# Scores one step ahead of the weighing in the router's attention of a graph and expert kernel

## What is computed

```
h = (x_flat @ W_gat).reshape(M, HEADS, NUM_EXPERTS)          # HEADS 4, NUM_EXPERTS 4
a_src, a_dst = (h * att_src).sum(-1), (h * att_dst).sum(-1)
e = leaky_relu(a_src[src] + a_dst[dst], negative_slope=0.2)
ee = exp(e - segment_max(e, dst)[dst])
alpha = ee / (segment_sum(ee, dst)[dst] + 1e-16)
agg = segment_sum(h[src] * alpha[:, :, None], dst) + b_gat
scores = layernorm(agg).mean over heads
w = softmax(top 2 of scores)
out = sum over experts of w * (gelu(x @ W1[ei] + b1[ei]) @ W2[ei] + b2[ei])
```

## Time and profile before

| | |
|---|---|
| median of three runs | 5306.82 us (5290.3 to 5312.11) |
| the profiled execution | 5308.64 us, its span 5307.1 us |
| mean granted clock of PE over the span | 0.876 of full speed |
| PE busy | 3317.8 us (63%) |
| DVE busy | 3019.0 us (57%) |
| POOL busy | 2063.6 us (39%) |
| ACT busy | 1600.5 us (30%) |
| exponentials of the router's attention (L2894) | 65 |
| indirect gathers of its rows (L2831) | 352 in 44 octets |

### The profile page before, as it was taken

How to read it: one execution, slowest core, us unless ns; L and a number is a source line. 1 busy time by engine, 2 the same in 40 slices (tenths; PEclk the granted TensorE clock), 3 DMA queues, 4 the chain that set the end, 5 groups by cost and what they waited for, 6 DMA issues and landing times. The chain is left out here.

```text
span 5307.1 us, 71457 instructions
## 1 busy us (share of the span) xinstructions
PE 3317.8 (63%) x17311; PEld 2482.2 (47%) x17312; DVE 3019.0 (57%) x7503; ACT 1600.5 (30%) x2745; POOL 2063.6 (39%) x1895
## 2 busy tenths in 40 slices
PE   0440036499698695277771699868345567777677
PEld 0430036487586584255550244356234445555455
DVE  8886648588588556133335754442444555565563
ACT  0232024376475121133330454322101222222221
POOL 1136300200200252656551200026377877777662
PEclk9999999899898796588885899979677788898899
DMA  0311125443452322211123554422443333333241
GB/s 31 74 19 44 13 82 232 169 153 104 170 159 85 111 67 91 88 27 33 33 38 108 200 170 158 165 91 67 129 91 86 88 86 83 82 84 84 78 76 28
DMA packets 326382, 501.17 MB, mean 94 GB/s; under 512 B 152614, under 2 KB 241005, under 8 KB 324168
## 3 DMA queue, kind: packets, MB, share of 16 engines
q1 hardware_dynamic: 193750, 259.75, 15.6%
q0 software_dynamic: 83888, 189.73, 13.7%
q10 hardware_dynamic: 48578, 49.98, 2.8%
HBM read 367.16 MB, written 137.35 MB: 95 GB/s over the span
## 5 line engine op out<-in xcount | busy, mean ns | idle before, releaser
L2393 POOL DMA_INDIRECT l3a_got<-rows,l3a_idx x832 | 1003.3, 1206 | 356.1 <-issue 257.5
L2469 PE MATMUL ps<-l3a_v,ident 128*128 x2032 | 592.9, 455 | 476.8 <-DVEq L2596 395.3
L2469 PEld LDWEIGHTS ps<-l3a_v,ident 128*128 128x128 f32 x2032 | 452.5, 228 | 614.5 <-issue 522.0
L1659 PE MATMUL ps<-l0a_all_rows,l0a_w 128*128 128x257 f32 x2500 | 559.5, 384 | 38.1 <-DVE l0a_w L1768 37.8
L1659 PEld LDWEIGHTS ps<-l0a_all_rows,l0a_w 128*128 128x128 f32 x2500 | 473.9, 191 | 124.3 <-issue 54.3
L2831 POOL DMA_INDIRECT l1a_got<-rows,l1a_idx x352 | 351.2, 998 | 248.8 <-DVEq L3033 130.0
L2069 PE MATMUL ps<-l2a_table,l2a_count 128*128 128x512 bf16 x1875 | 409.7, 382 | 38.1 <-ACT l2a_count L1994 38.1
L2419 ACT ACT_TABLE_LOAD x90 | 115.5, 1283 | 750.7 <-issue 459.4
L2854 PE MATMUL ps<-xt,l1w_w 128*128 x640 | 225.8, 506 | 169.3 <-ACT l1a_h L2909 74.2
L2069 PEld LDWEIGHTS ps<-l2a_table,l2a_count 128*128 128x128 bf16 x1875 | 183.9, 98 | 264.0 <-issue 46.6
L2590 DVE TENSOR_TENSOR l3a_v<-l3a_got,l3a_p_kept x127 | 291.6, 2296 | 0.0
(11 more groups left out here) (1019 smaller groups left out, 6446.8 us busy)
## 6 DMA issues: line engine op xcount, KB each, us to landing
l0a_held<-counts SPq DMA_DIRECT2D x130, 640.0 KB
counts<-count_held SPq DMA_DIRECT2D x13, 3200.0 KB
l2a_held<-counts SPq DMA_DIRECT2D x65, 640.0 KB
l3a_got<-rows,l3a_idx POOLq DMA_INDIRECT x832
l_y<-l1a_y_sb ACTq DMA_DIRECT2D x20, 640.0 KB
l2a_table<-rows SPq DMA_DIRECT2D x16, 640.0 KB, 5.1
l2a_state<-l1a_fresh ACTq DMA_DIRECT2D x1, 9984.0 KB
l2a_seen<-l2a_state POOLq DMA_DIRECT2D x12, 768.0 KB, 6.0
```

The source lines that it names most:

```text
L1659: ins = pe.matmul(sums_of(n, k, D + 1), w[:, at, k * P:(k + 1) * P], all_rows[:, at, 1:RW], start=(at == 0), stop=(at == HI - 1))
L2393: pool.indirect_dma_start(out=got[:, at:at + RW], out_offset=None, in_=rows[:, :], in_offset=bass.IndirectOffsetOnAxis(ap=idx[:, a, k:k + ...
L2469: ins = pe.matmul(totals, c.ident[:, :], rows_now[:, k, :, :].rearrange("p h d -> p (h d)"), start=(k == 0), stop=(k == ADDED - 1))
```

## The change

`edges` is cut in two, `scores_of` (L3008 to L3014 before) and `values_of` (L3018 to L3027). The scores of the opening step are followed at once by the emptying of PE's outputs. A loop step makes the scores of octet o and then the values of octet o-1; the values of the last octet follow behind the loop. The exponentials lie in `p_kept`, two tiles by turns, chosen by o % 2 in a register. `weighed` becomes `exped`: from the second step on DVE waits for the exponentials before it writes `d` anew, and once more behind the loop. `freed` is counted up behind the multiplication of an octet instead of at the entry of the next step.

```diff
-        e, d, p = (sb(n, [P, SLOTS + 1, H]) for n in ("e", "d", "p"))
+        e, d = (sb(n, [P, SLOTS + 1, H]) for n in ("e", "d"))
+        p_kept = sb("p_kept", [P, 2, SLOTS + 1, H])
...
+        def weights(o, lo, hi):
+
+            return p_kept[:, bass.ds(o % 2, 1), lo:hi, :].rearrange("p o s h -> p (o s) h")
...
-                    def exponentials():
+                    def exponentials(o):
                         act.wait_ge(shifted, 1)
                         act.sem_clear(shifted)
-                        act.activation(p[:, :, :], d[:, :, :], ACT.Exp).then_inc(weighed, 1)
+                        act.activation(weights(o, 0, SLOTS + 1), d[:, :, :], ACT.Exp).then_inc(exped, 1)
...
-                    def edges(o, row):
-                        ch.restart()
+                    def scores_of(o, row, opening):
...
                         ch(dve.tensor_reduce(top[:, :], e[:, :, :].rearrange("p s h -> p h s"), AX, ALU.max))
+                        if not opening:
+                            dve.wait_ge(exped, 1)
+                            dve.sem_clear(exped)
                         ch(dve.tensor_tensor(d[:, :, :], e[:, :, :], top[:, :].unsqueeze(1).broadcast_to([P, SLOTS + 1, H]), ALU.subtract))
                         dve.sem_inc(shifted, 1)
                         ch(dve.tensor_copy(e[:, SLOTS, :], top[:, :]))
 
-                        dve.wait_ge(weighed, 1)
-                        dve.sem_clear(weighed)
+                    def values_of(o, closing):
+
+                        if closing:
+                            dve.wait_ge(exped, 1)
+                            dve.sem_clear(exped)
+                        mine, older = weights(o, 0, SLOTS), weights(o, SLOTS, SLOTS + 1).rearrange("p s h -> p (s h)")
...
-                        ch.add(dve.tensor_tensor(by_head(acc), by_head(acc), spread(p[:, SLOTS, :]), ALU.mult))
+                        ch.add(dve.tensor_tensor(by_head(acc), by_head(acc), spread(older), ALU.mult))
                         ch.join()
-                        ch.add(dve.tensor_tensor(p[:, SLOTS, :], p[:, SLOTS, :], den, ALU.mult))
+                        if not closing:
+                            dve.sem_inc(freed, 1)
+                        ch.add(dve.tensor_tensor(older, older, den, ALU.mult))
...
-                    edges(begins // SLOTS, begins % SLOTS)
+                    first, last = begins // SLOTS, ends // SLOTS
+                    scores_of(first, begins % SLOTS, True)
                     beside()
-                    with dve.Fori(begins // SLOTS + 1, ends // SLOTS + 1) as o:
-                        dve.sem_inc(freed, 1)
-                        edges(o, closing_row(ends, o))
+                    with dve.Fori(first + 1, last + 1) as o:
+                        ch.restart()
+                        scores_of(o, closing_row(ends, o), False)
+                        values_of(o - 1, False)
+                    ch.restart()
+                    values_of(last, True)
```

More of the change, by code:

```diff
@@ L2780, in attend_beside_experts @@
         warmed, warm = sb("warmed", [P, 1]), sem("warm")
-        shifted, weighed, closed, kept, placed = (sem(n) for n in ("shifted", "weighed", "closed", "kept", "placed"))
+        shifted, exped, closed, kept, placed = (sem(n) for n in ("shifted", "exped", "closed", "kept", "placed"))
         product, hidden, used, emptied, y_out = (sem(n) for n in ("product", "hidden", "used", "emptied", "y_out"))
@@ L2889, in attend_tile @@
                 def attend_tile(t, at):
-                    def exponentials():
+                    def exponentials(o):
                         act.wait_ge(shifted, 1)
                         act.sem_clear(shifted)
-                        act.activation(p[:, :, :], d[:, :, :], ACT.Exp).then_inc(weighed, 1)
+                        act.activation(weights(o, 0, SLOTS + 1), d[:, :, :], ACT.Exp).then_inc(exped, 1)
                     begins, ends = stream.bounds(act, t)
-                    exponentials()
+                    exponentials(begins // SLOTS)
                     at(0)
                     with act.Fori(begins // SLOTS + 1, ends // SLOTS + 1) as o:
-                        exponentials()
+                        exponentials(o)
                     at(1)
@@ L3014, in edges @@
                         ch(dve.tensor_copy(e[:, SLOTS, :], top[:, :]))
-                        dve.wait_ge(weighed, 1)
-                        dve.sem_clear(weighed)
+                    def values_of(o, closing):
[3 more added lines that the diff above has]
+                        mine, older = weights(o, 0, SLOTS), weights(o, SLOTS, SLOTS + 1).rearrange("p s h -> p (s h)")
                         ch.add(dve.tensor_tensor(v[:, :, :].rearrange("p s (h d) -> p s h d", h=H),
                                                  buffer(o, 0, VW).rearrange("p s (h d) -> p s h d", h=H),
-                                                 p[:, 0:SLOTS, :].unsqueeze(3).broadcast_to([P, SLOTS, H, DH]), ALU.mult))
-                        ch.add(dve.tensor_tensor(by_head(acc), by_head(acc), spread(p[:, SLOTS, :]), ALU.mult))
+                                                 mine.unsqueeze(3).broadcast_to([P, SLOTS, H, DH]), ALU.mult))
+                        ch.add(dve.tensor_tensor(by_head(acc), by_head(acc), spread(older), ALU.mult))
                         ch.join()
-                        ch.add(dve.tensor_tensor(p[:, SLOTS, :], p[:, SLOTS, :], den, ALU.mult))
+                        if not closing:
+                            dve.sem_inc(freed, 1)
+                        ch.add(dve.tensor_tensor(older, older, den, ALU.mult))
                         ch.add(dve.tensor_reduce(part[:, :], v[:, :, :].rearrange("p s w -> p w s"), AX, ALU.add))
                         ch.join()
-                        ch.add(dve.tensor_reduce(den, p[:, :, :].rearrange("p s h -> p h s"), AX, ALU.add))
+                        ch.add(dve.tensor_reduce(den, weights(o, 0, SLOTS + 1).rearrange("p s h -> p h s"), AX, ALU.add))
                         ch.add(dve.tensor_tensor(acc, acc, part[:, :], ALU.add))
```

## The result

The change makes the kernel slower: 5330.72 us against 5305.87, a ratio of 1.0053 with a 95% interval of 1.0038 to 1.0067. The forecast was 5277. The profiled execution took 5342.05 us (span 5340.5), 33 more than the one of before, and all of it lies in the stage of the change: it ran from about 2176.5 to 2855.6.

What follows compares the result with a forecast made beforehand. No engine was full; a ring of waits among PE, ACT and DVE bound the stage. Gains 5.0 + 20.4 + 5.0 + 1.3 = 31.7 took 5306.82 to 5275; 2 back for register work gave 5277 us, range 5256 to 5303.

Steps and rivals of the forecast that it cites:

- PE's waits before the outputs: PE's idle before L2865, 53.4 us in all; earlier exponentials were to save 20.4 us of it.
- the higher clock: PE's 20-matmul runs behind three long waits return from 6.1 to 6.2 us to 4.55: 5.0 us gained.
- The other two terms: Tiles without a turn, four counted, gain 5.0 us; the last tile, whose end starts the closing gather, gains 1.3 us.
- just enough: At a tile's last step, older values and loop exit give 1.8 us of cover for the exponential's wait.
- Priced 0: DVE's free signal comes 2.2 to 2.5 us later at POOL's 25 waits; claimed to cost nothing.
- cover of 20 us: Gathers begun at 2399.69 serve an octet DVE took up at 2434.87: over 20 us of room for later frees.
- they seem tied to the place in the program, so they would move along: Argument against the stops rival: PE's 60.5 us of "issue" gaps before L2854 would shift with the program.
- eaten by PE's own stops: Rival: PE's unreleased gaps end at their own times, halving 25 us of the turns' gain; 5290 us, chance 0.26.
- The slower rival: Buffers freed too late: each of POOL's 25 waits passes on 2.5 us; 5339 us, chance 0.04.
- the 130 us of waits: POOL's 25 waits for DVE's freed buffers, read as gathers running ahead; held against the slower rival.
- The page: Skill page adding about 1.38 us drain per ACT table switch, 2.66 in all; by it the gain is about 25.
- The range: Forecast from 5256 us (more comes back, upper bounds) to 5303 us (gain nearly all eaten, 0.25 us register work a step).

Runs made afterwards that it cites:

- e1: Kernel before, with freed counted up only behind a loop step's scores and exponentials, about 2 us later; 5380 us, ratio 1.0081 to before.
- e3: Changed kernel, with POOL waiting behind each octet's eight gathers until they have landed; 5306 us, ratio 0.9949 to before.
- e13: The changed kernel itself, without further edit, measured again where the kernel before took 5099 us; 5071 us, ratio 0.9945 to before.
- sets 3 to 5: Later sets of runs, in which the unedited kernel before took 5096 us, then 5099 us in the other two.
- sets 0 to 2: First sets of runs, in which the unedited kernel before took 5306, 5337 and 5343 us.

## Why the prediction was wrong

- **The order of the work: right.** The sum was 31.7, with 2 taken back. Without stops it measures 28.9, 30.3 and 29.4 us with half the gathers, 27.9 with all. PE's waits before the outputs were to give 20.4 and gave 25.1 (42.8 to 17.7); the higher clock was to give 5.0 back, and the same 800 matmuls were 4.8 shorter (187.8 to 183.0). The other two terms were not measured apart, so the close sum is in part luck. The multiplication keeps 16.2 us of wait behind ACT, 0.8 in each of 20 places, where I had called the cover "just enough": it was 0.8 to 1.0 short at the last step of a tile with a turn.
- **The failed step: "Priced 0", of the later free signal.** Its cover of 20 us was the right one for landings, and landings indeed did not come late. But the signal also sets when POOL's gathers start beside PE's turn. Alone it cost 43 us (e1), more than the sum. The runs of gathers were as long as before; 22 of PE's signals for hidden rows fell into their later octets in place of 10, and eight times nothing went on until the run was over. In its condition, -29 and +43 would leave +14; measured were +28 (20 to 36). The three figures come from different sets, so the parts may add or not.
- **A wrong cause that cost nothing: "they seem tied to the place in the program, so they would move along", of PE's stops.** They are tied to POOL's runs: e3, which breaks the runs, has none, nor has e13. But in amount they did what was said, 56.5 us before and 57.5 after. Part of the 60.5 us that I read as such stops was a wait for ACT without a record (7.0). I had the rows, stops of up to 7 us without a releaser and a register instruction of 704 ns in the earlier trace rows where 125 is usual, and did not ask what POOL did then; that question would have led to the free signal.
- **The rival "eaten by PE's own stops"** did not come: these stops were as long as before. The gain was lost in PE's waits for ACT (131.6 to 161.5), which itself waited for PE's late signals.
- **The slower rival** had the right signal and sign and the wrong way: no landing was late, and "the 130 us of waits" that I held against it speak of landings alone.
- **The page.** The Trainium skill, "ScalarE: Activation LUTs", section "What ACT_TABLE_LOAD costs", would add a drain of about 1.38 us to a switch. This case's trace does not agree: in e13 and in the changed kernel each load took 1.283 us, it began 0.02 us behind the activation before it where ACT had not to wait, and the exponential behind it 0.01 us after its end. e13's waits behind ACT last at most 1.0 us, in a place with 1.8 us of cover.
- **The range** rested on one set of runs. In the condition of sets 3 to 5 the forecast of -0.56% is met (0.9945); in that of sets 0 to 2, which was the one shown, it isn't.

## What to carry to other kernels

A signal that frees a buffer does two things: it lets data come, and it sets when the engine that fetches them is busy beside the others. Before pricing its delay at nothing, lay the producer's runs beside the idle without a releaser on all engines; where such idle ends just behind a run, moving the run is a change of the time. Where the profile lacks the record of a signal, an ordinary wait looks like such idle: see first what the awaited engine did just ahead. And where idle time has no releaser, measure the change's two parts apart before believing either, and in more than one set of runs: here the sign turned between sets.

## What the runs showed of the hardware

- In sets 0 to 2, beside indirect DMAs issued by POOL every 1.30 us, from 10.7 us behind the start of a run on (sooner only where the pause ahead of it was 2.3 us or less), register, branch and semaphore instructions of DVE and SP took 0.70 us or twice that. PE's weight loads came 0.70 or 1.40 us apart 14 times before and 26 times in the change, never in e13. The arithmetic kept its durations. At 1.89 us a gather two such instructions were left in this stage, with 2.4 us of pause behind every eight gathers one.
- In the same sets PE's signals were recorded up to 33.6 us behind its last matmul beside runs at 1.30 us a gather, and all engines but POOL stood for 5 to 11 us, until 2 to 4 us behind the run's last gather (eight times in e1). At 1.89 us a gather, and in sets 3 to 5 at 1.30 us, every recorded signal of PE was there within 0.02 us.
- In sets 3 to 5 the same programs showed neither, and before was 207 to 247 us faster as a whole: 80 of it lies ahead of this stage, about 100 in it (an estimate, from the 485 us of before with half the gathers and the 15 us between the two in time). For the change 143 us lie in it (629 and 486). Before showed such instructions from 488 to 658 us too, beside other gathers.
- Why a signal of PE is held up, and whether the 0.70 us instructions have the same cause, no run here tells.
